# First GAT aggregation on one core: VectorE takes two of the five PSUM banks of every finished head, ScalarE the other three

## The chip, the cores and the metric

The kernel runs on one core of one Trainium2 chip. The metric is device time in microseconds (us), the median of the runs. A core has five engines with queues of their own: TensorE (PE, the matmuls; PEld is its weight load), VectorE (DVE), ScalarE (ACT), GpSimd (POOL) and SyncE (SP, which here only starts transfers). They meet through semaphores: an instruction raises a semaphore when it is done, and another engine's queue waits for a value.

## The reference, cut to what matters

A graph with 1250 nodes and 20000 edges goes through two residual blocks with a layernorm each. The first block is three graph attention layers with four heads of 192 channels, side by side, so twelve heads in all:

```python
def gat_conv(x, src, dst, W, a_src, a_dst, b):
    h = (x @ W).reshape(N, H, C)                      # N 1250, H 4, C 192
    e = leaky_relu(as_n[src] + ad_n[dst], 0.2)
    p = exp(e - segment_max(e, dst)[dst])
    s = segment_sum(p, dst)
    alpha = p / (s[dst] + 1e-16)
    out = segment_sum(alpha[:, :, None] * h[src], dst)
    return out.reshape(N, H * C) + b
xs = [relu(gat_conv(x1, src, dst, W, a_s, a_d, b)) for three sets of weights]
x = layernorm(x + relu(concat(xs) @ W_out + b_out))
```

The second block is two more attention layers. The change touches only the aggregation (the last two lines of gat_conv) of the first block.

## The kernel before

The edges are kept as a dense matrix of counts: CT holds, for ten tiles of 125 source nodes, how many edges go to each of the 1250 destinations. The sum over the edges of a head is then a product of a 1250 x 1250 matrix p with the head's rows h. The stage is the function aggregate_layer0. Its loop has ITERS = 6 iterations of two heads (hh = 0 and 1; together 384 columns, PAIR), each of 10 source tiles, so 20 steps g an iteration and 120 blocks in all.

- For a block, ScalarE makes two 125x1250 exponentials (L1081: e<-first_room,col for the first head of a pair, e<-uv,col for the second, each of which it announces by exp_ready). VectorE takes their maximum (L1119) and multiplies its cut-off value by the counts (L1124), which gives p. TensorE multiplies the ten 125x125 pieces of p with h_in (125x193: 192 channels and a column of ones, which gives the divisor s); each of the ten f32 products shows as two records in the trace, so 20 a block, and 200 a head (L1183). p has RING = 4 slots, e as well: VectorE can be up to four blocks ahead of TensorE.
- The ten destination tiles of a head gather in PSUM in p_o, two tiles to a bank, BANKS = 5 banks, over all ten blocks. The first matmul that a new head puts into a bank waits until that bank has been read out (bank_free).
- When a head is finished, VectorE works out the divisors (the helper divisors): adds 1e-16 and takes the reciprocal, for banks 0 and 1 when TensorE has finished those (banks_done), then for banks 2 to 4 when the whole head is done (L1108 and L1112, twice each). In its queue this stands behind the p of the second block of the next head (g == NT + 1, and g == 1 of the next iteration).
- ScalarE reads the ten tiles out, times their reciprocal, into res (leave_head, L1051), each two tiles raising bank_free by one. In its queue this stands behind the exponentials of the fourth block of the next head. Tiles 0 to 3 wait for the first divisors, tiles 4 to 9 for the second.
- In the first head of a pair (blocks g = 1, 3, 5) TensorE also turns the finished pair round by 10 transposes each time (turn, L1165, into p_t), and ScalarE adds the bias and applies relu behind g = 5, 7, 9 (keep, L1066); the exponentials that follow in ScalarE's queue come after it. SP stores the result (L1008). At the very end VectorE does the last third (L1144).
- The last head of the stage is an exception before the change: there ScalarE reads out only BY_ACT = 6 tiles, and VectorE the tiles 6 to 9 (L1138), with the semaphore last_left.
- VectorE also does work for a later stage in between: in 16 of the 120 blocks, every seventh (g + 20i = 4, 11, 18, ...), two reductions of 128x768 (L653, wa_by). 

The order within an engine is written out by hand; there is no planner.

Of the kernel before, what the change touches and what calls it, by code (L numbers as in the profile page):

```python
# [10 lines left out]
ALU = mybir.AluOpType  # L11
# [7 lines left out]
NT = N // T  # L19
# [9 lines left out]
H0, C0 = 4, 192  # L29
CONVS = 3  # L30
PAIR = 2 * C0
# [884 lines left out]
def aggregate_layer0(nc, core, h_rows, col_src, bias, turned_rows, w2, a2, w_out):  # L916
# [4 lines left out]
    ITERS = CONVS * H0 // 2  # L921
    STEPS = 2 * NT
    BANKS = 5
    FIRST = 2
    CW = PAIR // 128
    RING = 4
    with ExitStack() as ctx:
        sb, pb, sem = core.tools(ctx)
# [6 lines left out]
        res = sb("res", [T, NT, PAIR], F32)  # L935
        sums = sb("sums", [T, 2, NT], F32)
# [6 lines left out]
        p_o = p_all[0:T]  # L943
# [10 lines left out]
        sum_steps = sem("sum_steps")  # L954
        bank_free = sem("bank_free")
        turned = sem("turned")
        out_ready = sem("out_ready")
        stored = core.turned0_stored
        last_left = sem("last_left")
        last_out = sem("last_out")  # L960
        mask_saved = sem("mask_saved")
        ahead_in = sem("ahead_in")
        weighed = ScoreWeights(nc, sb, sem, "wa2_by", 2, D // 2, 2, K1, K1, 1)
        BY_ACT = 6

        def place(i, c):

# [68 lines left out]
        @block.scalar  # L1036
        def _(act):
            a = nc.scalar
            for c in range(CW):
                a.sem_inc(stored[c], 16)  # L1040
            a.sem_inc(bank_free, BANKS)

            def leave_head(i, hh, tiles=NT):

                act.wait_ge(turned, i * CW + CW)
                for d in range(tiles):
                    if d == 0:
                        act.wait_ge(sum_steps, (i * 2 + hh) * 4 + 2)
                    if d == 2 * FIRST:
                        act.wait_ge(sum_steps, (i * 2 + hh) * 4 + 4)  # L1050
                    last = a.activation(res[:, d, hh * C0:(hh + 1) * C0], p_o[:, d // 2, (d % 2) * 256:(d % 2) * 256 + C0],  # L1051
                                        ACT.Copy, scale=sums[:, 1, d:d + 1])
                    if d % 2:
                        last.then_inc(bank_free, 1)

            def keep(i, c):
                if i == 0 and c == 0:
                    act.wait_ge(bias_in, 16)
                    act.wait_ge(core.uv_late, all_uv)
                    act.wait_ge(core.h0_stored[0], all_h)  # L1060
                    act.wait_ge(core.h0_late, 64)
                act.wait_ge(turned, i * CW + (c + 1 + CW))

                wait_apart(act, stored[c], i * 16 + 16)
                for b, k in ((0, 4), (1, 4), (2, 2)):
                    last = a.activation(out_f[:, c, 4 * b * T:(4 * b + k) * T], place(i, c)[:, b, 0:k * T], ACT.Relu,  # L1066
                                        bias=b_col[:, bass.ds(i, 1), c])
                last.then_inc(out_ready, 1)

            def body(i, first):  # L1070
                for g in range(STEPS):
                    hh, s = divmod(g, NT)
                    if s == 0:
                        if g == 0:
                            wait_apart(act, core.first_uv_in if first else uv_in[0], 64 if first else i * 64)
                        else:
                            wait_apart(act, uv_in[1], i * 64 + 64)

                    wait_apart(act, p_ready, i * STEPS + (g + 1))
                    for kind in range(2):  # L1080
                        last = a.activation(e[:, g % RING, kind, :], uv[hh][:, kind, :], ACT.Exp,  # L1081
                                            bias=col_src[kind][:, bass.ds(i * 2 + hh, 1), s])
                    last.then_inc(exp_ready, 1)
                    if g == NT + 3:
                        leave_head(i, 0)
                    if g == 3 and not first:
                        leave_head(i - 1, 1)
                    if g in (5, 7, 9) and not first:
                        keep(i - 1, (g - 5) // 2)

            every_iteration(act, body)
            leave_head(ITERS - 1, 1, BY_ACT)
            for c in range(CW - 1):
                keep(ITERS - 1, c)

        @block.vector
        def _(dve):
            v = nc.vector
            v.sem_inc(p_ready, RING)
            v.sem_inc(exp_ready, 2 * NT)  # L1100

            def divisors(i, hh):
                for n, (b0, b1) in enumerate(((0, FIRST), (FIRST, BANKS))):
                    if n == 0:
                        dve.wait_ge(banks_done, i * 2 + hh + 1)
                    else:
                        dve.wait_ge(p_used, i * STEPS + ((hh + 1) * NT + 2 * NT))
                    v.tensor_scalar(sums[:, 0, 2 * b0:2 * b1].rearrange("p (b n) -> p b n", n=2),  # L1108
                                    p_o[:, b0:b1, :].rearrange("p b (n c) -> p b n c", n=2)[:, :, :, C0],
                                    1e-16, None, ALU.add).then_inc(sum_steps, 1)  # L1110
                    dve.wait_ge(sum_steps, (i * 2 + hh) * 4 + 2 * n + 1)
                    v.reciprocal(sums[:, 1, 2 * b0:2 * b1], sums[:, 0, 2 * b0:2 * b1]).then_inc(sum_steps, 1)  # L1112

            def body(i, first):
                for g in range(STEPS):
                    hh, s = divmod(g, NT)
                    dve.wait_ge(exp_ready, i * STEPS + (g + 1 + 2 * NT))

                    v.tensor_tensor(e[:, g % RING, 0, :], e[:, g % RING, 0, :], e[:, g % RING, 1, :], ALU.max).then_inc(more_ready, 1)  # L1119
                    dve.wait_ge(more_ready, i * STEPS + (g + 1))  # L1120

                    dve.wait_ge(p_used, i * STEPS + (g + 1 + 2 * NT - RING))

                    v.scalar_tensor_tensor(p[:, g % RING, :], e[:, g % RING, 0, :], 1.0, CT[:, s, :],  # L1124
                                           ALU.min, ALU.mult).then_inc(p_ready, 1)
                    if (i * STEPS + g) % 7 == 4 and (i * STEPS + g) // 7 < K1:
                        k = (i * STEPS + g) // 7
                        weighed.reduce(dve, k, lambda kind, j: core.wa2[:, k, kind:kind + 1])
                    if g == NT + 1:
                        divisors(i, 0)  # L1130
                    if g == 1 and not first:
                        divisors(i - 1, 1)

            every_iteration(dve, body)
            divisors(ITERS - 1, 1)
            dve.wait_ge(sum_steps, ITERS * 8)
            for d in range(BY_ACT, NT):
                last = v.tensor_scalar(res[:, d, C0:PAIR], p_o[:, d // 2, (d % 2) * 256:(d % 2) * 256 + C0], sums[:, 1, d:d + 1],  # L1138
                                       None, ALU.mult)
            last.then_inc(last_left, 1)  # L1140
            dve.wait_ge(turned, ITERS * CW + CW)
            dve.wait_ge(stored[CW - 1], ITERS * 16)
            for b, k in ((0, 4), (1, 4), (2, 2)):
                last = v.tensor_scalar(out_f[:, CW - 1, 4 * b * T:(4 * b + k) * T], p_t[:, b, 0:k * T],  # L1144
                                       b_col[:, ITERS - 1, CW - 1:CW], 0.0, ALU.add, ALU.max)
            last.then_inc(last_out, 1)

        @block.tensor
        def _(pe):
# [1 line left out]
            nc.tensor.sem_inc(turned, CW)  # L1151

            def turn(i, c):
                if i == ITERS - 1:
                    if c == 0:
                        pe.wait_ge(bank_free, i * (2 * BANKS) + 2 * BANKS + BY_ACT // 2)
                        pe.wait_ge(last_left, 1)
                    if c == 2:
                        pe.wait_ge(out_ready, i * CW + 1)
                elif c:  # L1160
                    pe.wait_ge(out_ready, i * CW + c)
                else:
                    pe.wait_ge(bank_free, i * (2 * BANKS) + 3 * BANKS)
                for d in range(NT):
                    last = nc.tensor.transpose(place(i, c)[:, d // 4, (d % 4) * T:(d % 4 + 1) * T],  # L1165
                                               res[:, d, c * 128:(c + 1) * 128], ident[0:T, 0:T])
                last.then_inc(turned, 1)

            def body(i, first):
                for g in range(STEPS):  # L1170
# [7 lines left out]
                    for d in range(NT):  # L1178
                        b, n = divmod(d, 2)
                        if s == 0 and n == 0:  # L1180

                            pe.wait_ge(bank_free, i * (2 * BANKS) + (BANKS * hh + b + 1))
                        last = nc.tensor.matmul(p_o[:, b, n * 256:n * 256 + C0 + 1], p[:, g % RING, d * T:(d + 1) * T],  # L1183
                                                h_in[hh][:, s, 0:C0 + 1], start=(s == 0 and n == 0), stop=(s == NT - 1),
                                                skip_group_check=True)
# [1620 lines left out]
```

## Time and profile before

| | before |
|---|---|
| median of 3 runs | 1889.95 us (1888.43 to 1895.02) |
| profiled execution | 1893.19 us, of which the span on the core 1891.5 us |
| PE, PEld | 1801.7 us (95%), 1742.3 us (92%) |
| VectorE | 1454.5 us (77%) |
| ScalarE | 981.8 us (52%) |
| POOL | 130.7 us (7%) |
| stage of the change | about 430 to 862 us of the span |

The profile is of one execution. An idle time is put down to what ended it. The chain of waits that ended last shows only the last 129 us of the span, which says nothing of this stage; the stage has to be read from its own stretch of the trace.

### The profile page before, as it was taken

The numbers are of one execution on the slowest core, as the hardware profiler recorded it, in microseconds if no ns is written. First come the engines' busy times: TensorE is split into PE (matmuls) and PEld (weight loads), VectorE is DVE, ScalarE is ACT, GpSimd is POOL, SyncE is SP. The second block draws the span as 40 slices with busy tenths as digits, with TensorE's granted clock in tenths as the row PEclk, the third lists the DMA queues.
The fourth block names the chain that finished last, engine by engine and source line by source line (L and its number), as shares of the span: only waits on it lengthen the run. The fifth ranks groups of instructions, "written<-read, shape, count | busy, mean of one in ns | idle before, by whom it ended". The sixth has DMA issues, their size and how long they took to land. (4 is left out here: it accounts for less than half of the span.)

```text
span 1891.5 us, 30185 instructions
## 1 busy us (share of the span) xinstructions
PE 1801.7 (95%) x11151; PEld 1742.3 (92%) x11151; DVE 1454.5 (77%) x2514; ACT 981.8 (52%) x1535; POOL 130.7 (7%) x133
## 2 busy tenths in 40 slices
PE   7999899997999999997999899989999998999898
PEld 6877699997999999996999899989999998999898
DVE  7888599998888988984645549658999995356766
ACT  5766421217898898874211232236677764232633
POOL 3110201201000000000011111100000000000000
PEclk9999899999999999998999999989999998999999
DMA  4221345454464535538654385572442408444302
GB/s 128 71 63 54 99 107 152 102 137 118 130 147 106 124 92 118 137 61 204 187 177 147 106 234 172 152 202 84 140 139 79 141 28 247 123 130 123 99 11 82
DMA packets 179272, 234.11 MB, mean 124 GB/s; under 512 B 75943, under 2 KB 151655, under 8 KB 178889
## 3 DMA queue, kind: packets, MB, share of 16 engines
q1 hardware_dynamic: 170407, 202.98, 39.6%
q0 software_dynamic: 7984, 27.24, 5.1%
q10 hardware_dynamic: 748, 2.10, 0.4%
q8 instruction: 85, 1.39, 0.3%
q14 instruction: 48, 0.39, 0.1%
HBM read 167.27 MB, written 65.00 MB: 123 GB/s over the span
## 5 line engine op out<-in xcount | busy, mean ns | idle before, releaser
L1849 PE MATMUL p_o<-p_hi,h_parts 125*128 125x416 f32 (+1 forms) x960 | 277.1, 356 | 9.4 <-DMA h_parts<-h_rows 7.8
L1183 PE MATMUL p_o<-first_room,p 125*125 125x193 f32 x1200 | 202.0, 329 | 10.4 <-DVE p L1124 7.5
L1183 PEld LDWEIGHTS p_o<-first_room,p 125*125 125x125 f32 x1200 | 197.2, 189 | 11.9 <-issue 11.4
L1183 PE MATMUL p_o<-h_in,p 125*125 125x193 f32 x1200 | 199.8, 329 | 2.1 <-ACT res L1051 2.1
L1183 PEld LDWEIGHTS p_o<-h_in,p 125*125 125x125 f32 x1200 | 197.6, 189 | 3.6 <-issue 2.4
L1849 PEld LDWEIGHTS p_o<-p_hi,h_parts 125*128 125x128 f32 x960 | 182.3, 190 | 16.1 <-DMA h_parts<-h_rows 8.3
L800 DVE CUSTOM_DVE_ANT_0 max_junk<-src_row,G 125x1250 bf16<-125x1250 f32 x120 | 184.8, 1611 | 3.7 <-ACT src_row L838 1.6
L1119 DVE TENSOR_TENSOR e<-e 125x1250 f32<-125x1250 f32 x120 | 174.3, 1452 | 17.2 <-ACT e L1081 17.1
L904 PE MATMUL p_h<-pw_hi,x1T 128*125 128x384 f32 x720 | 187.3, 341 | 0.0
L1124 DVE SCALAR_TENSOR_TENSOR p<-e,CT 125x1250 f32<-125x1250 f32 x120 | 175.3, 1461 | 4.6 <-PE p_o L1183 0.4
L1519 PE MATMUL p_h<-pw_hi,x2T 128*125 128x256 f32 (+1 forms) x960 | 175.1, 284 | 0.4 <-DVE h_out L1475 0.4
L1849 PE MATMUL p_o<-p_lo,h_parts 125*128 125x416 f32 (+1 forms) x480 | 170.4, 355 | 0.0
L1081 ACT ACTIVATE e<-first_room,col 125x1250 f32<-125x1250 f32 x120 | 151.0, 1344 | 3.9 <-DVE p L1124 2.5
L1081 ACT ACTIVATE e<-uv,col 125x1250 f32<-125x1250 f32 x120 | 149.0, 1349 | 1.2 <-DVE p L1124 1.2
L1519 PEld LDWEIGHTS p_h<-pw_hi,x2T 128*125 128x125 f32 x960 | 148.2, 187 | 0.7 <-DVE h_out L1475 0.7
L1519 PE MATMUL p_h<-pw_lo,x2T 128*125 128x256 f32 (+1 forms) x480 | 135.7, 283 | 0.0
L2120 PE MATMUL p_y<-fw_hi,f_hi 128*125 128x384 f32 x360 | 123.4, 343 | 10.4 <-DVE fw_lo L2044 10.4
L904 PEld LDWEIGHTS p_h<-pw_hi,x1T 128*125 128x125 f32 x720 | 131.6, 188 | 1.2 <-POOL pw_lo L781 1.2
L2120 PE MATMUL p_y<-fw_hi,f_lo 128*125 128x384 f32 x360 | 122.9, 341 | 0.0
L2120 PE MATMUL p_y<-fw_lo,f_hi 128*125 128x384 f32 x360 | 122.9, 341 | 0.0
L904 PE MATMUL p_h<-pw_lo,x1T 128*125 128x384 f32 x360 | 122.5, 340 | 0.0
L2401 PE MATMUL p_y<-fw_hi,f_hi 128*125 128x386 f32 x320 | 111.2, 347 | 11.1 <-DVE fw_lo L2301 5.6
(292 smaller groups left out, 3730.0 us busy)
## 6 DMA issues: line engine op xcount, KB each, us to landing
f_raw<-turned SPq DMA_DIRECT2D x40, 500.0 KB, 8.9
h_parts<-h_rows SPq DMA_DIRECT2D x40, 448.0 KB
turned<-tail_room SPq DMA_DIRECT2D x18, 625.0 KB, 6.6
G<-turned SPq DMA_DIRECT2D x20, 562.5 KB
h_rows<-tail_room SPq DMA_DIRECT2D x22, 424.4 KB
h_rows<-h_out SPq DMA_DIRECT2D x16, 560.0 KB
h_rows<-tail_room SPq DMA_DIRECT2D x14, 560.0 KB
first_room<-in_w_gat POOLq DMA_DIRECT2D x36, 192.0 KB, 2.7
```

Of the source, the lines that this page charges most:

```text
L800: v.tensor_tensor_reduce(out=junk[:, t % 2, :], in0=src_row[:, h % 2, :], in1=G[:, t, :], scale=1.0, scalar=NO_EDGE, op0=ALU.subtract, op1 ...
L904: last = nc.tensor.matmul(p_h[:, (u * NT + t) % 4, 0:width], xp[:, k, at], wp[:, u, k, :], start=(k == 0 and n == 0), stop=(k == KD - 1 an ...
L1081: last = a.activation(e[:, g % RING, kind, :], uv[hh][:, kind, :], ACT.Exp, bias=col_src[kind][:, bass.ds(i * 2 + hh, 1), s])
L1119: v.tensor_tensor(e[:, g % RING, 0, :], e[:, g % RING, 0, :], e[:, g % RING, 1, :], ALU.max).then_inc(more_ready, 1)
L1124: v.scalar_tensor_tensor(p[:, g % RING, :], e[:, g % RING, 0, :], 1.0, CT[:, s, :], ALU.min, ALU.mult).then_inc(p_ready, 1)
L1183: last = nc.tensor.matmul(p_o[:, b, n * 256:n * 256 + C0 + 1], p[:, g % RING, d * T:(d + 1) * T], h_in[hh][:, s, 0:C0 + 1], start=(s == 0 ...
L1519: last = nc.tensor.matmul(p_h[:, n % 4, 0:width], xp[:, k, at], wp[:, q % 2, k, 0:width], start=(k == 0 and j == 0), stop=(k == KD - 1 and ...
L1849: last = nc.tensor.matmul(p_o[:, bank(n, c), 0:w], h[:, s, kind, cols].bitcast(F32R), pp[:, g % RING, 0:w], start=(s == 0 and j == 0), sto ...
L2120: last = nc.tensor.matmul(p_y[:, t % 2, half, 0:CW], fp[:, n % 2, kk, :], wp[:, k, cols], start=(k == 0 and j == 0), stop=(k == KO - 1 and ...
L2401: last = nc.tensor.matmul(p_y[:, t % 2, 0:CW + 2], fp[:, m % 2, kk, :], wp[:, k, :], start=(k == 0 and j == 0), stop=(k == K1 - 1 and j == 2))
```

## The change

In every finished head, not only in the last one, ScalarE reads out the six tiles of banks 0 to 2, and VectorE the four tiles of banks 3 and 4, right behind the second reciprocal. ScalarE counts its banks in bank_free, VectorE its own in bank_left, and TensorE waits for the one or the other by the bank's number. The special case of the last head and last_left are gone.

```diff
+        ACT_BANKS, DVE_BANKS = BY_ACT // 2, BANKS - BY_ACT // 2
...
-            a.sem_inc(bank_free, BANKS)
-
-            def leave_head(i, hh, tiles=NT):
+            a.sem_inc(bank_free, ACT_BANKS)
+
+            def leave_head(i, hh):
 
                 act.wait_ge(turned, i * CW + CW)
-                for d in range(tiles):
+                for d in range(BY_ACT):
...
-            leave_head(ITERS - 1, 1, BY_ACT)
+            leave_head(ITERS - 1, 1)
...
+            v.sem_inc(bank_left, DVE_BANKS)
...
                     v.reciprocal(sums[:, 1, 2 * b0:2 * b1], sums[:, 0, 2 * b0:2 * b1]).then_inc(sum_steps, 1)
+                dve.wait_ge(turned, i * CW + CW)
+                dve.wait_ge(sum_steps, (i * 2 + hh) * 4 + 4)
+                for d in range(BY_ACT, NT):
+                    last = v.tensor_scalar(res[:, d, hh * C0:(hh + 1) * C0], p_o[:, d // 2, (d % 2) * 256:(d % 2) * 256 + C0],
+                                           sums[:, 1, d:d + 1], None, ALU.mult)
+                    if d % 2:
+                        last.then_inc(bank_left, 1)
...
             divisors(ITERS - 1, 1)
-            dve.wait_ge(sum_steps, ITERS * 8)
-            for d in range(BY_ACT, NT):
-                last = v.tensor_scalar(res[:, d, C0:PAIR], p_o[:, d // 2, (d % 2) * 256:(d % 2) * 256 + C0], sums[:, 1, d:d + 1],
-                                       None, ALU.mult)
-            last.then_inc(last_left, 1)
...
             def turn(i, c):
-                if i == ITERS - 1:
-                    if c == 0:
-                        pe.wait_ge(bank_free, i * (2 * BANKS) + 2 * BANKS + BY_ACT // 2)
-                        pe.wait_ge(last_left, 1)
-                    if c == 2:
-                        pe.wait_ge(out_ready, i * CW + 1)
-                elif c:
+                if c == 0:
+                    pe.wait_ge(bank_free, (i * 2 + 3) * ACT_BANKS)
+                    pe.wait_ge(bank_left, (i * 2 + 3) * DVE_BANKS)
+                elif i < ITERS - 1:
                     pe.wait_ge(out_ready, i * CW + c)
-                else:
-                    pe.wait_ge(bank_free, i * (2 * BANKS) + 3 * BANKS)
+                elif c == 2:
+                    pe.wait_ge(out_ready, i * CW + 1)
...
-                            pe.wait_ge(bank_free, i * (2 * BANKS) + (BANKS * hh + b + 1))
+                            if b < ACT_BANKS:
+                                pe.wait_ge(bank_free, (i * 2 + hh) * ACT_BANKS + b + 1)
+                            else:
+                                pe.wait_ge(bank_left, (i * 2 + hh) * DVE_BANKS + b - ACT_BANKS + 1)
```

## Rows read from the trace of the kernel before

**Rows 1.** The stage: span, busy PE, PEld, DVE, ACT, POOL, then clock, DMA, GB/s.
```profile
430.00:862.00 432.00, 417.83 (x2580) 414.00 (x2580) 378.56 (x357) 361.47 (x407) 16.17 (x23) 0.99 0.48 113
```

**Rows 2.** Waits in 430 to 862 us: who for whom, sum, times, longest.
```profile
DVE sums L1108 <- PE p_o L1183: 28.3, 15, 7.6
DVE e L1119 <- ACT e L1081: 17.1, 10, 5.9
PE p_o L1183 <- ACT res L1051: 5.0, 4, 2.1
PEld p_o L1183 <- ACT res L1051: 1.7, 7, 0.2
```

**Rows 3.** Timeline of PE: start, duration, count, idle before it, releaser.
```profile
472.90 34.59 PE L1183 MATMUL p_o<-h_in,p 125*125 125x193 f32 x200 [2.12 <-ACT res L1051]
...
613.38 33.04 PE L1183 MATMUL p_o<-h_in,p 125*125 125x193 f32 x200
647.39 6.77 PE L1183 MATMUL p_o<-first_room,p 125*125 125x193 f32 x40 [0.96 <-ACT res L1051]
...
753.31 33.05 PE L1183 MATMUL p_o<-h_in,p 125*125 125x193 f32 x200
786.19 6.91 PE L1183 MATMUL p_o<-first_room,p 125*125 125x193 f32 x40
```

**Rows 4.** Timeline of DVE and ACT between iterations 2 and 3.
```profile
644.66 1.46 DVE L1124 SCALAR_TENSOR_TENSOR p<-e,CT 125x1250 f32<-125x1250 f32 x1
646.04 0.16 DVE L1108 TENSOR_SCALAR sums<-p_o 125x4 f32<-125x4 f32 x1
...
646.51 3.23 ACT L1051 ACTIVATE res<-p_o,sums 125x192 f32<-125x192 f32 x10 [5.19 <-DVE sums L1112]
646.66 0.19 DVE L1112 RECIPROCAL sums<-sums 125x6 f32<-125x6 f32 x1
646.77 1.42 DVE L1119 TENSOR_TENSOR e<-e 125x1250 f32<-125x1250 f32 x1
```

**Rows 5.** Groups in 430 to 862 us: count, busy us, mean ns, idle before.
```profile
L653 DVE CUSTOM_DVE_ANT_1 wa_by_junk<-wa_by_w,wa_by_a 128x768 bf16<-128x768 f32 x32 | 29.3, 952 | 0.5 <-DMA wa_by_w<-in_w 0.5
```

**Rows 6.** Timeline of DVE between iterations 4 and 5.
```profile
784.43 0.16 DVE L1108 TENSOR_SCALAR sums<-p_o 125x4 f32<-125x4 f32 x1
```

**Rows 7.** Timeline of ACT, DVE and PEld from 600 to 615 us, iteration 2.
```profile
600.62 1.61 ACT L1066 ACTIVATE tail_room<-p_t,b_col 128x500 f32<-128x500 f32 x3 [1.10 <-PE p_t L1165]
604.70 1.46 DVE L1119 TENSOR_TENSOR e<-e 125x1250 f32<-125x1250 f32 x1 [1.78 <-ACT e L1081]
611.62 0.16 DVE L1108 TENSOR_SCALAR sums<-p_o 125x4 f32<-125x4 f32 x1 [1.09 <-PE p_o L1183]
613.89 1.42 DVE L1119 TENSOR_TENSOR e<-e 125x1250 f32<-125x1250 f32 x1
614.79 6.34 PEld L1183 LDWEIGHTS p_o<-h_in,p 125*125 125x125 f32 x39 [0.24 <-ACT res L1051]
```

**Rows 8.** Timeline of DVE between iterations 0 and 1, and at the stage's end.
```profile
505.57 0.16 DVE L1108 TENSOR_SCALAR sums<-p_o 125x4 f32<-125x4 f32 x1 [2.49 <-PE p_o L1183]
...
855.79 1.39 DVE L1138 TENSOR_SCALAR res<-p_o,sums 125x192 f32<-125x192 f32 x4
```

**Rows 9.** Timeline of PE: two other idle times of this size.
```profile
857.33 1.26 PE L1165 MATMUL p_t<-ident,res 125*128 125x125 f32 x10 [2.00 <-DVE res L1138]
...
1613.24 0.41 PE L2401 MATMUL p_y<-fw_hi,f_hi 128*125 128x386 f32 x1 [2.42 <-DVE f_lo L2296]
```

**Rows 10.** Busy time by stretch, as in rows 1, behind four idle times.
```profile
473.90:476.90 3.00, 3.00 (x11) 3.00 (x10) 2.96 (x3) 3.00 (x7) 0.00 (x0) 0.50 0.86 234
648.40:651.40 3.00, 3.00 (x21) 3.00 (x20) 2.96 (x3) 3.00 (x7) 0.00 (x0) 1.00 0.72 235
858.30:861.30 3.00, 2.26 (x21) 2.03 (x20) 0.00 (x0) 2.57 (x5) 0.00 (x0) 1.00 0.02 5
1614.24:1617.24 3.00, 3.00 (x11) 3.00 (x10) 1.02 (x3) 0.00 (x0) 0.00 (x0) 0.50 0.98 259
```

More of the change, by code:

```diff
@@ L958, in aggregate_layer0 @@
         stored = core.turned0_stored
-        last_left = sem("last_left")
+        bank_left = sem("bank_left")
         last_out = sem("last_out")
```

## The prediction

> **What bounds the kernel now.** The change touches one stage, so I read the trace by stage, and not by the whole span's shares (VectorE 77%, ScalarE 52%), which average over other stages. The busy time of the stage comes first [rows 1]: of 432 us TensorE is busy 417.8, VectorE 378.6, ScalarE 361.5. TensorE is the bound, but VectorE has only some 12% to spare, and ScalarE 16%. The sum of waits comes next [rows 2]: TensorE waits for ScalarE's read-outs (line 1051) for 5.0 us in 4 places, and its weight load for 1.7 us more in 7. That is all the change can win here, 6.7 us. VectorE waits 28.3 us for TensorE and 17.1 us for exponentials: that is the slack on which an addition to VectorE has to draw. Last the timeline [rows 3, 4, 7], for the one question that matters: when a head is done, who is late?
>
> There are two kinds of head change. Behind the first head of a pair VectorE is early: at 611.62 it has waited 1.09 us for TensorE, and TensorE goes on at 613.38 without an idle time [rows 3, 7]. Behind the second head it is late. At 646.04 it starts the divisors straight from its last p, with no wait [rows 4]; ScalarE starts at 646.51, has the second tile out at about 646.51 + 0.31 + 0.43 = 647.25 (ten tiles in 3.23 us), and TensorE starts at 647.39, having been idle 0.96 us [rows 3]. So from VectorE's divisors to TensorE's start it is 1.35 us, and that chain runs through bank 0: first divisors, tiles 0 and 1. It is seen at the ends of iterations 1, 2 and 3 (one row of the three stands). At the end of iteration 4 it is nearly level: divisors at 784.43, TensorE goes on at 786.19 with no idle row [rows 3, 6].
>
> **The change part by part.**
>
> *ScalarE's four tiles taken away* (0.31 us each, 1.3 us a head). The tiles are those of banks 3 and 4. The wait at the late change ends with tile 1, in bank 0, and the small wait of 0.24 us in the other heads [rows 7] ends with tiles 4 and 5, in bank 2: it is 0.64 us of matmuls for two banks after the head's start. Both stay with ScalarE, behind the same divisors. Banks 3 and 4 are reached by TensorE some 2 us after its start, and were free by then already: ScalarE frees a bank in 0.62 us, TensorE fills one in 33.04/50 = 0.66 us. Gain on TensorE: 0. ScalarE's later exponentials come 1.3 us earlier, but no one waits for them there: VectorE's waits for exponentials are in the first head of a pair, behind ScalarE's bias step, which itself waited 1.10 us for TensorE's transposes [rows 7]. Gain: 0.
>
> *VectorE's four tiles added* to 11 more heads (the twelfth, the last of the stage, has them already). Four take 1.39 us [rows 8]. Before, the next maximum started 0.08 us ahead of the recorded end of the second reciprocal (646.66 + 0.19 against 646.77) [rows 4]; a read-out that waits for that reciprocal can't, so I take 1.45. The bounds are 1.39, and 1.75 if in the midst of the stage they do not overlap (four of 0.41, and 0.1 for the waits), for the row is from a moment in which TensorE is still. The waits on turned and sum_steps find their values there, the first one long ago. Queued behind them on VectorE are the next block's maximum and p; TensorE has two finished blocks then (6.6 us of matmuls), VectorE needs 1.45 + 2.9 us for the next, so no block comes late. What comes late is the next divisors, when VectorE has no slack on the way to them.
>
> *First heads of a pair (five).* VectorE has 1.78 us of waiting for the exponentials of the last block but one before the divisors [rows 7], set by TensorE's transposes through the bias step, so 1.45 us are swallowed; and behind that there are another 1.09 us of waiting. Cost 0. Iteration 5 has two reductions in that head and only just fits into these two. The end of iteration 0 has 2.49 us of waiting [rows 8]: cost 0.
>
> *Second heads with two pairs of reductions on the way (iterations 1, 2, 3).* PE starts at 613.38, VectorE goes on at 613.89 and has no wait until the divisors at 646.04. Now it goes on at 615.34 and is there at 647.49; TensorE starts at 647.49 + 1.35 = 648.84 in place of 647.39. All 1.45 us come through, and the idle time grows from 0.96 to 2.41 us. Three times 1.45 = 4.35 us.
>
> *Second head with one pair (iteration 4).* A pair of reductions costs 29.3/16 = 1.8 us [rows 5]. By the same path VectorE is there 0.51 + 32.15 - 1.8 = 30.9 us after TensorE's start at 753.31, so at 784.2 (it began at 784.43), now at 785.6, and TensorE starts at 787.0 in place of 786.19. The small wait in bank 2 goes (6.91 against 6.77 us for 40 records [rows 3]). Net 0.65 us. The ends of iteration 0's first head and of the last head stay as they are.
>
> Without the clock the sum is 4.35 + 0.65 = +5.0 us (bounds 3 x 1.39 + 0.5 = 4.7 and 3 x 1.75 + 0.95 = 6.2).
>
> *The clock.* The head that starts at 472.90 behind an idle time of 2.12 us takes 34.59 us for its 200 records, against 33.04 for the same head of iteration 2 [rows 3], and the granted clock behind it is 0.50, that is 1.2 instead of 2.4 GHz; behind 0.96 us of idle it stays at 1.00 [rows 10]. So one fall costs 1.55 us. The three idle times grow to 2.41 us, from the size that left the clock alone to the size at which it fell. Of the other idle times near that, 2.42 us was followed by 0.50, and 2.00 us, in front of two short runs of transposes, by 1.00 [rows 9, 10]. Two fell of three, and the nearest in size and surroundings (dense matmuls on both sides) both fell: 0.8 for each. Three falls are likeliest: 3 x 1.55 = +4.65 us. The Trainium skill (TensorE: Matmul & The Clock Gate, section on HAM oscillation) gives as its rule that the clock is lost only behind longer idle times than any of these. The trace does not agree, at 2.12 and 2.42 us; by the page the sum would stay without this term.
>
> Together +9.65 us. The profiled execution would go from 1893.19 (span 1891.5, and 1.7 around it) to 1902.8. That execution is 3.2 us over the median, inside the runs' spread, so I put the difference on the median: 1889.95 + 9.65 = **1899.6 us**.
>
> **The rivals.**
> - *Fewer falls.* One or two of the three: +6.5 to +8.1 us, 1896.5 to 1898.1. Chance 0.27.
> - *The clock stands,* which is where the page's rule leads: VectorE's lateness is all, +5.0, 1894.95. For it speaks the 2.00 us that left the clock at 1.00. Chance 0.10.
> - *The other side: the read-out itself is what TensorE waits for.* If a head change waits for all five banks and not for bank 0, two engines at once end it sooner, and the waits on line 1051 go: up to -6.7 us, 1883.3. It decides from the point where TensorE's start follows the tenth tile. In the profile it follows the second by 0.14 us, while the tenth ends at 649.74, so this has 0.06, and most of that for a small part of the gain.
> - *VectorE's lateness is swallowed also in second heads,* through ScalarE's 1.3 us. That needs a wait of VectorE for exponentials between 613.89 and 646.04, and the trace has none; -1 to +3, about 1891. Chance 0.07.
> - *First heads become late as well,* if the read-out takes over 2 us beside TensorE's writes: 1.4 us more in four heads, and more falls: +15, 1905. Chance 0.05.
>
> **How the numbers follow.** Forecast 0.45, rivals 0.27, 0.10, 0.06, 0.07, 0.05. About 0.3% (5.7 us) is what a measurement of this kernel can tell from no change. Slower by more: 0.45 + 0.27 + 0.05, less 0.05 for one fall, which lies close to the bound: 0.72. Within: 0.25. Faster: 0.03. The range leaves out the last rival and the two with gains: from 1893.5 (no fall, less the scatter) to 1904.0 (three falls with the upper bound of the read-out, 6.2 + 4.65 = 10.9, and 3 us of scatter).
>
> **What would show it.** In the profile after: four VectorE instructions from p_o to res in each of twelve heads, at a pitch near 0.33 us; ScalarE's 72 of them; TensorE's idle time 2.4 us in three places and 0.8 us in one, at the ends of iterations 1 to 4, and none new behind first heads; granted clock 0.50 behind the three, and heads of 35 us there; VectorE's waits for TensorE and for exponentials smaller by together some 10 us. The prediction is wrong if the idle times stay at 0.96 us, if the clock stays at 1.00, or if the read-outs take over 0.5 us each.

## The result and the profile after

| | before | after |
|---|---|---|
| median of 9 runs | 1893.17 us (1888.43 to 1896.81) | 1901.23 us (1897.59 to 1905.12) |
| ratio | | 1.0046 (95% interval 1.0034 to 1.0058), that is +6.4 to +11.0 us |
| profiled execution, its span | 1893.19, 1891.5 us | 1901.74, 1900.0 us |
| VectorE, ScalarE busy | 1454.5, 981.8 us | 1469.5, 969.9 us |

The change makes the kernel slower by 8 to 9 us, 0.46%; the interval does not reach down to no change. It does what it says: VectorE has 48 read-outs in place of 4, ScalarE 72 in place of 116. The stage from its first matmul to the next stage's first grew from 432.7 to 440.2 us, +7.4 of the +8.5 us between the two spans.

The busy time of the stage's stretch in the kernel after, columns as in rows 1, and two stretches behind idle times of TensorE:

```profile
430.00:862.00 432.00, 416.83 (x2550) 413.42 (x2550) 391.66 (x396) 345.70 (x355) 16.17 (x23) 0.98 0.46 113
650.00:653.00 3.00, 3.00 (x10) 3.00 (x11) 2.96 (x5) 3.00 (x6) 0.00 (x0) 0.50 0.86 245
...
723.50:726.50 3.00, 3.00 (x21) 3.00 (x20) 2.97 (x3) 3.00 (x5) 0.00 (x0) 1.00 0.87 240
```

VectorE's busy time went up by 13.1 us in this stretch, ScalarE's down by 15.8. The two were at 378.6 and 361.5 [rows 1] and are further apart now: VectorE was the fuller one already. The timeline of TensorE in the kernel after tells the rest (start, duration, records, idle time before and its releaser):

```profile
472.37 32.91 PE L1187 MATMUL p_o<-h_in,p 125*125 125x193 f32 x200 [0.86 <-ACT res L1052]
...
576.73 8.45 PE L1187 MATMUL p_o<-first_room,p 125*125 125x193 f32 x40 [2.49 <-ACT res L1052]
...
614.37 33.05 PE L1187 MATMUL p_o<-h_in,p 125*125 125x193 f32 x200
649.90 8.34 PE L1187 MATMUL p_o<-first_room,p 125*125 125x193 f32 x40 [2.48 <-ACT res L1052]
...
722.96 6.77 PE L1187 MATMUL p_o<-first_room,p 125*125 125x193 f32 x40 [2.48 <-ACT res L1052]
...
792.69 6.77 PE L1187 MATMUL p_o<-first_room,p 125*125 125x193 f32 x40 [0.73 <-ACT res L1052]
...
864.97 2.29 PE L1166 MATMUL p_o<-ident,res 125*128 125x125 f32 x10
```

The three idle times of 0.96 us [rows 3] are now 2.48 us, and there is a fourth of 0.73 us where there was none. Behind two of the four the first 40 records take 8.4 in place of 6.77 us: the granted clock there is 0.50, that is 1.2 GHz. Behind the third of 2.48 us it stayed at 1.00.

What VectorE and ScalarE do at such a place, and at the end of the first head of the same iteration (lines 1110 and 1114 are the divisors, 1118 VectorE's read-out, 1052 ScalarE's, 1128 the next block's maximum):

```profile
605.69 1.46 DVE L1128 TENSOR_TENSOR e<-e 125x1250 f32<-125x1250 f32 x1 [1.78 <-ACT e L1082]
612.61 0.16 DVE L1110 TENSOR_SCALAR sums<-p_o 125x4 f32<-125x4 f32 x1 [1.10 <-PE p_o L1187]
```

```profile
614.77 0.19 DVE L1114 RECIPROCAL sums<-sums 125x6 f32<-125x6 f32 x1
615.00 0.73 ACT L1052 ACTIVATE res<-p_o,sums 125x192 f32<-125x192 f32 x2 [0.56 <-DVE sums L1114]
615.07 1.39 DVE L1118 TENSOR_SCALAR res<-p_o,sums 125x192 f32<-125x192 f32 x4
...
615.78 1.27 PEld L1187 LDWEIGHTS p_o<-h_in,p 125*125 125x125 f32 x8 [0.24 <-ACT res L1052]
616.38 1.45 DVE L1128 TENSOR_TENSOR e<-e 125x1250 f32<-125x1250 f32 x1
```

```profile
648.56 0.16 DVE L1110 TENSOR_SCALAR sums<-p_o 125x4 f32<-125x4 f32 x1
...
649.03 1.98 ACT L1052 ACTIVATE res<-p_o,sums 125x192 f32<-125x192 f32 x6 [5.19 <-DVE sums L1110]
...
649.31 1.46 DVE L1118 TENSOR_SCALAR res<-p_o,sums 125x192 f32<-125x192 f32 x4
649.87 3.33 PEld L1187 LDWEIGHTS p_o<-first_room,p 125*125 125x125 f32 x11 [2.75 <-issue]
```

In the first head VectorE's waits at 605.69 and 612.61 are 1.78 and 1.10 us, as before (1.78 and 1.09 [rows 7]): the addition was swallowed by then. In this head the clock had fallen, which gave VectorE time as well. Where it stood, in the first head of iteration 4, the waits for exponentials were 1.18 and 1.78 us before, and one of 1.68 us is left; from start to start of TensorE this head takes 35.95 us, before 35.96. Before, then after:

```profile
729.43 1.46 DVE L1119 TENSOR_TENSOR e<-e 125x1250 f32<-125x1250 f32 x1 [1.18 <-ACT e L1081]
...
737.03 1.46 DVE L1119 TENSOR_TENSOR e<-e 125x1250 f32<-125x1250 f32 x1 [1.78 <-ACT e L1081]
```

```profile
742.63 1.46 DVE L1128 TENSOR_TENSOR e<-e 125x1250 f32<-125x1250 f32 x1 [1.68 <-ACT e L1082]
```

Over the stretch VectorE's waits for TensorE and for exponentials shrank from 28.3 and 17.1 us [rows 2] to 22.4 and 13.9, together by 9.1. The small wait of the weight load in bank 2 is also the same 0.24 us, and it ends with ScalarE's read-out; VectorE's banks come later and nobody waits for them. In the second head VectorE goes on 2.01 us behind TensorE's start (614.37 to 616.38) and not 0.51 [rows 3, 7], has no wait on the way, and reaches the divisors 34.19 us behind it (648.56), in place of 32.66. TensorE starts 1.34 us later, at 649.90.

The working by heads, from start to start of TensorE, after against before: ends of iterations 1, 2, 3: +1.53, +1.52, +1.52; end of iteration 4: +0.90, less 0.14 for the wait in bank 2. That is +5.3 us of lateness. Falls of the clock: +1.68 and +1.58 behind two of the three places, -1.68 because the fall behind rows 3's 2.12 us did not come this time (the very first head, 35.69 in place of 34.67 us, was slower by a longer stretch at half clock, and the idle time behind it only 0.86 us), and +0.7 for the last transposes (2.29 us for ten, in place of 1.23). With -0.2 from the very first head and its wait, and +0.1 at the end of the last head, that is the +7.4.

### The profile page after: what moved, and what is told of

Its sections match the earlier page's. It is cut to its first block and busy times, and to the rows that moved or that the text cites. A ratio compares the mean times of both kernels' runs of the same rounds, so it can differ in the third digit from the quotient of the medians.

```text
span 1900.0 us, 30203 instructions
## 1 busy us (share of the span) xinstructions
PE 1804.1 (95%) x11151; PEld 1744.7 (92%) x11151; DVE 1469.5 (77%) x2558; ACT 969.9 (51%) x1491; POOL 131.0 (7%) x133
## 3 DMA queue, kind: packets, MB, share of 16 engines
q8 instruction: 85, 1.39, 0.3%
## 5 line engine op out<-in xcount | busy, mean ns | idle before, releaser
L1187 PE MATMUL p_o<-first_room,p 125*125 125x193 f32 x1200 | 206.1, 334 | 15.7 <-ACT res L1052 8.2
L1187 PEld LDWEIGHTS p_o<-first_room,p 125*125 125x125 f32 x1200 | 201.4, 192 | 17.2 <-issue 17.0
L1128 DVE TENSOR_TENSOR e<-e 125x1250 f32<-125x1250 f32 x120 | 174.5, 1455 | 14.0 <-ACT e L1082 13.9
```

## The experiments

Theory: the only cost is VectorE's lateness at the divisors, where it has no slack on its way, plus what TensorE's clock loses behind the longer idle times; relieving ScalarE is worth nothing. Rivals: TensorE waits for the read-out as a whole; or reading PSUM from two engines costs in itself; or the clock plays no part. Ratios are to the kernel before, run beside each, with their 95% intervals. A fall of the clock means that the granted clock behind an idle time of TensorE is 0.50, in place of 1.00.

**e1_relief_only.** Only the relief of ScalarE: the kernel leaves out VectorE's read-outs in eleven heads. In addition it sets their tiles to zero once at the start (not shown).

```diff
                 dve.wait_ge(sum_steps, (i * 2 + hh) * 4 + 4)
+                if (i, hh) != (ITERS - 1, 1):
+                    v.sem_inc(bank_left, DVE_BANKS)
+                    return
                 for d in range(BY_ACT, NT):
```

> The kernel after, but VectorE's four read-outs of a head are left out in the first eleven heads (tiles 6 to 9 of res stay zero there, so part of the result is missing); banks 3 and 4 are handed back right behind the second reciprocal. ScalarE keeps its six tiles, so only the relief of ScalarE is left of the change. My theory (VectorE's lateness at the divisors is the whole cost, ScalarE's relief is worth nothing): TensorE's idle time at the ends of iterations 1 to 3 is 0.96 us as before, the time is that of the kernel before within 2 us. Rival (TensorE waits for the read-out of the whole head): the idle times go below 0.3 us, the time is 3 to 7 us under the kernel before.

Measured: 0.9999 (0.9983 to 1.0016), no change within 3 us. TensorE's timeline at the end of iteration 2, with VectorE's next maximum:

```profile
645.35 1.46 DVE L1134 TENSOR_TENSOR e<-e 125x1250 f32<-125x1250 f32 x1
...
645.92 2.36 PE L1193 MATMUL p_o<-first_room,p 125*125 125x193 f32 x13 [1.22 <-ACT res L1053]
```

ScalarE has 40% less to read out, and the kernel is not faster: the relief is worth nothing, and the first rival falls. The idle time is 1.22 and not the 0.96 us that I had expected. Of these 0.26 us the waits and the raise of the semaphore that stayed make 0.21: at the end of the first head the next maximum starts 0.32 us behind the start of the second reciprocal (612.06 to 612.38), before 0.11.

**e2_extra_only.** VectorE's time alone: the kernel before, and VectorE spends 1.38 us in SBUF (not shown: the buffer extra is set to zero once at the start).

```diff
                     v.reciprocal(sums[:, 1, 2 * b0:2 * b1], sums[:, 0, 2 * b0:2 * b1]).then_inc(sum_steps, 1)
+                if (i, hh) != (ITERS - 1, 1):
+                    n = i * 2 + hh + 1
+                    dve.wait_ge(spent, n)
+                    v.tensor_tensor(extra[:, 1, :], extra[:, 0, :], extra[:, 0, :], ALU.max).then_inc(spent, 1)
```

> The kernel before, ScalarE reads out all ten tiles as there, and VectorE does one additional maximum of 1210 columns in SBUF (about 1.4 us) behind the second reciprocal of the first eleven heads, whose result nobody uses. My theory: the same as the kernel after, idle times of 2.4 us at the ends of iterations 1 to 3 and about 0.8 us at the end of iteration 4, +5.0 us and 1.55 us more for each fall of the clock, so +5 to +10 us. Rival (it is the reading of PSUM by VectorE, or two engines reading it at once, that costs): idle times 0.96 us, time of the kernel before.

Measured: 1.0047 (1.0032 to 1.0062), which is the kernel after's 1.0046, with no change to who reads PSUM.

```profile
649.97 3.23 ACT L1053 ACTIVATE res<-p_o,sums 125x192 f32<-125x192 f32 x10 [5.18 <-DVE sums L1111]
650.06 1.38 DVE L1119 TENSOR_TENSOR extra<-extra 125x1210 f32<-125x1210 f32 x1
...
650.84 3.34 PE L1190 MATMUL p_o<-first_room,p 125*125 125x193 f32 x19 [2.29 <-ACT res L1053]
```

The idle times are 2.29, 2.29, 2.28 and 0.54 us. The rival of PSUM falls: idle times of 0.96 us and the time of the kernel before were its sign, and VectorE's time costs as much when VectorE spends it away from PSUM.

**e3_one_bank and e4_three_banks.** The dose.

```diff
-        BY_ACT = 6
+        BY_ACT = 8      # e3; in e4: 4
```

> The kernel after with VectorE taking one bank (two tiles) of each head in place of two, ScalarE eight tiles. VectorE's addition is 0.33 + 0.41 + 0.06 = 0.8 us. My theory: idle times of 0.96 + 0.8 = 1.76 us at the ends of iterations 1 to 3, 0.1 us or none at the end of iteration 4, +2.4 us over the kernel before, and 1.55 for each fall of the clock; at 1.76 us I expect fewer falls than at 2.41, one or two: +2.4 to +5.5. Last head: ScalarE reads eight tiles there too, some 0.3 us later. Rival (the cost is not proportional to the tiles, but comes with the second waiting engine): +8 us as in the kernel after.

> The kernel after with VectorE taking three banks (six tiles), ScalarE four. VectorE's addition is 5 x 0.33 + 0.41 + 0.06 = 2.1 us. My theory: idle times of 0.96 + 2.1 = 3.1 us at the ends of iterations 1 to 3 and 1.4 us at the end of iteration 4, so 3 x 2.1 + 1.3 = +7.6 us over the kernel before, and with three falls of the clock +12.2 us. Rival (cost not proportional to the tiles): +8 us as in the kernel after.

Measured: one bank 1.0018 (1.0008 to 1.0029), three banks 1.0083 (1.0056 to 1.0110). TensorE behind iteration 2, first of one bank, then of three:

```profile
648.70 6.77 PE L1187 MATMUL p_o<-first_room,p 125*125 125x193 f32 x40 [1.84 <-ACT res L1052]
```

```profile
654.91 2.04 DVE L1118 TENSOR_SCALAR res<-p_o,sums 125x192 f32<-125x192 f32 x6
...
655.51 6.77 PE L1187 MATMUL p_o<-first_room,p 125*125 125x193 f32 x40 [3.05 <-ACT res L1052]
```

Idle times of 0.96, 1.84, 2.48 and 3.05 us for zero, one, two and three banks: 0.88 us for the first bank, 0.64 and 0.57 for the next two. So 0.6 us is the price of two more tiles, and some 0.25 us that of having the block of read-outs at all, as e1 shows too. With one bank the clock fell behind none of the three places (I had expected one or two falls), and +3.4 us (1.5 to 5.5) fits 3 x 0.88 and a little. With three banks +15.7 us (10.6 to 20.8) is above my 12.2, inside the interval. The stage alone grew by 15.6 us in the profile. The lateness is 8.0 of them, near my 7.6, and there were two falls in the three places and not three, 3.4 us. What I had left out is the very first head change (an idle time of 3.52 us, and a head of 35.98 in place of 34.59 us behind it, together 2.7 us) and the end of the stage (an idle time of 2.72 us before the last transposes, and those partly at half clock, together 1.5 us). The heads themselves take 33.13 in place of 33.05 us: bank 2 is VectorE's now, and TensorE's weight load waits 0.32 us for it, where it waited 0.24 us for ScalarE's read-out.

**e5_before_moved.** The kernel before, with only the reductions for the later stage in other places.

```diff
-                    if (i * STEPS + g) % 7 == 4 and (i * STEPS + g) // 7 < K1:
-                        k = (i * STEPS + g) // 7
+                    if i * STEPS + g in REDUCE_AT:
+                        k = REDUCE_AT.index(i * STEPS + g)
```
```diff
+        REDUCE_AT = (16, 24, 28, 36, 44, 48, 56, 64, 68, 76, 84, 88, 96, 104, 108, 116)
```

> The kernel before; only the places of VectorE's 16 reductions for the later stage are changed: none in the first head, two in each later first head of a pair (behind the blocks 4 and 8), one in each second head (behind block 16) in place of two in three of them. My theory (TensorE is late where VectorE reaches the divisors late, and that is where two reductions lie on its way through a head without slack): the idle times at the ends of iterations 1 to 3 fall from 0.96 to 0, that at the end of the very first head from 2.12 us to at most 0.4, so -5 us, -6.5 us with the clock's fall behind 2.12 us: 0.25 to 0.35% faster than the kernel before. Rival (the idle times belong to ScalarE's read-out, not to VectorE's place): idle times and time as before.

Measured: 0.9968 (0.9954 to 0.9981), 6 us faster than the kernel before. TensorE at the end of the very first head and of iteration 1:

```profile
469.12 33.05 PE L1184 MATMUL p_o<-h_in,p 125*125 125x193 f32 x200
...
570.97 6.90 PE L1184 MATMUL p_o<-first_room,p 125*125 125x193 f32 x40
```

No idle time is left at a head change in the whole stage. This shows the cause from the other side: the same read-outs, the same divisors, the same number of instructions, only VectorE is there in time. It is the fastest kernel of this study.

**e6_after_moved.** The same for the kernel after.

```diff
+        REDUCE_AT = (4, 13, 17, 24, 28, 44, 48, 64, 68, 84, 88, 104, 108, 112, 114, 116)
```

> The kernel after with the reductions placed so that the second heads of iterations 1 to 4 hold none (first head one, second head of iteration 0 two, five first heads two each, last head three). My theory: VectorE gains 3.6 us or 1.8 us on its way to the divisors there against 1.45 us of read-outs, so the idle times at the ends of iterations 1 to 4 are all gone, and with them the falls of the clock: 8 to 11 us under the kernel after, 1 to 4 us under the kernel before; the last head may end up to 0.8 us later. Rival (the split read-out costs in itself, in every head): it stays 3 us or more over the kernel before.

Measured: 0.9988 (0.9975 to 1.0001), 11 us under the kernel after. The idle times behind iterations 1 to 4 are gone, but not all that I expected went:

```profile
505.25 6.77 PE L1188 MATMUL p_o<-first_room,p 125*125 125x193 f32 x40 [2.30 <-ACT res L1053]
...
834.20 6.80 PE L1188 MATMUL p_o<-h_in,p 125*125 125x193 f32 x40 [0.42 <-DVE p L1134]
841.70 10.07 PE L1188 MATMUL p_o<-h_in,p 125*125 125x193 f32 x60 [0.69 <-DVE p L1134]
```

In the second head of iteration 0 the read-out (1.5) and a second pair of reductions (1.8) stood against a slack of 2.49 us [rows 8]; that slack I had read from a profile in which TensorE ran this head 1.7 us slower by the clock (34.59 against 32.91 us here), and so much less was there. In the last head, which holds three pairs of reductions, TensorE waits twice for p, 1.1 us together, where I had allowed 0.8. The result is in the range, by a sum that was off in these two places; against the kernel before it is no clear gain. That the split read-out costs 3 us or more in every placing is refuted. The 4 us between this kernel and e5's are about the size of these idle times (2.30 + 0.42 + 0.69); a better placing of the reductions was not tried.

**e7_fill, e8_after_again, e9_fill_again.** TensorE waits busily: the kernel after, with transposes of the identity in the three waits. e8 is the kernel after itself, beside e9.

```diff
                     pe.wait_ge(p_ready, i * STEPS + (g + 1 + RING))
+                    if g == 0 and i in (2, 3, 4):
+                        pe.wait_ge(out_ready, (i - 1) * CW)
+                        for n in range(FILL):       # 18
+                            nc.tensor.transpose(p_t[0:T, 0, 0:T], ident[0:T, 0:T], ident[0:T, 0:T])
```

> The kernel after; at the ends of iterations 1 to 3 TensorE does 18 transposes of the identity (about 1.9 us) into a free bank of p_t in front of its wait, so it waits busily; nothing of the computation is changed. My theory (part of the cost is the fall of TensorE's clock behind 2.4 us of idle time): the new head starts at the same moment as in the kernel after, the granted clock stays at 1.00 there, each of the three heads takes its 6.77 us for the first 40 records and not 8.4, and the time is 1.55 us less for each fall avoided: 3 to 5 us under the kernel after, +4 to +5 over the kernel before. Rival (the clock plays no part): time of the kernel after.

> The kernel after once more, on the same chip and in the same rounds as the next two, so that they can be compared with it. VectorE's lateness (idle times of 2.48, 2.48, 2.48 and 0.73 us, +5.3 us) is the same in every run; the falls of the clock are not. So far the clock fell behind five of nine idle times of 2.1 to 2.5 us in this stage. My theory: +5.3 and 1.7 to 3 us for the falls, ratio 1.0035 to 1.0050.

> The same kernel as e7_fill (18 transposes of the identity in the three waits of TensorE), now beside the kernel after. Theory: the new heads start as late as in the kernel after, the clock stays at 1.00 behind them, 1.7 to 5 us under the kernel after. Rival (the clock is worth nothing in the sum of many runs): within 1 us of the kernel after.

Measured: filled 1.0020 (1.0009 to 1.0031) and again 1.0016 (1.0003 to 1.0030); the kernel after beside the second 1.0050 (1.0035 to 1.0065). TensorE in e7, end of iteration 2:

```profile
644.85 2.12 PE L1183 MATMUL p_t<-ident 125*125 125x125 f32 x18
647.40 6.80 PE L1192 MATMUL p_o<-first_room,p 125*125 125x193 f32 x40 [0.43 <-ACT res L1053]
```

From the second head's start (611.97) it is 35.43 us to 647.40, in the kernel after 35.53: the head starts only 0.1 us earlier than there. But its first 40 records take 6.80 and not 8.4 us, in all six filled places. So VectorE's lateness is all but untouched, and a part of the cost is gone: 4.9 and 6.4 us by the ratios, 5.3 and 3.9 by the medians (of the two pairs only the second ran side by side). That the clock plays no part is refuted: the intervals of e8 and e9 do not overlap. The size is less sure. In the profiles of the kernel after (twice) the clock fell behind 3 of 6 idle times of 2.48 to 2.49 us, which is 1.5 x 1.65 = 2.5 us a run; the gain by the ratios is larger, with an interval of 3 to 4 us to either side.

**e10_before_fill.** The same trick for the one fall in the kernel before.

```diff
+                    if first and g == NT:
+                        for n in range(FILL):       # 16
+                            nc.tensor.transpose(p_t[0:T, 0, 0:T], ident[0:T, 0:T], ident[0:T, 0:T])
```

> The kernel before with 16 transposes of the identity in TensorE's wait behind the very first head, where it is idle for 2.12 us. VectorE's place is unchanged, so the second head starts as late as before. Theory: only the fall of the clock behind that wait goes, which comes in some runs: -0.5 to -1.7 us, hardly more than can be measured; in the profile the second head takes 33.0 us and not 34.6. Rival (the busy wait itself delays the head): the second head starts later than 1.35 us behind VectorE's divisors.

Measured: 0.9996 (0.9986 to 1.0007), no difference that the time can tell, as expected. In the profile:

```profile
470.74 1.91 PE L1181 MATMUL p_t<-ident 125*125 125x125 f32 x16
473.68 32.94 PE L1187 MATMUL p_o<-h_in,p 125*125 125x193 f32 x200 [1.03 <-ACT res L1052]
```

The head takes 32.94 in place of 34.59 us [rows 3], the idle time before it being 1.03 and not 2.12 us. The wait itself was longer in this run (2.94 us in all), so that the two together say nothing on the total. It was VectorE that was later: it starts the divisors at 472.43, 0.9 us later than in the kernel before. TensorE follows 1.25 us behind, before 1.34 us, so the busy wait itself does not delay the head.

## Why the prediction was right, and where it was off

- *Direction and size.* 1899.6 us was forecast, 1901.2 measured, in the range of 1893.5 to 1904.0. The difference was forecast as +9.65 us and is +8.1 by the medians, +8.7 by the ratio. That the absolute number fits is in part luck: the median of before is 3.2 us higher over nine runs than over the three that I had, and that made up for a difference forecast 1.0 to 1.6 us too large.
- *ScalarE's relief: 0.* Right (e1), and for the reason given: both waits of TensorE end in banks 0 and 2, which ScalarE keeps. One figure on the way was wrong: two banks of matmuls are 2 x 0.66 = 1.3 us, not 0.64, which fits bank 2 better still (the weight load waits until 614.79, 1.41 us behind the head's start at 613.38 [rows 3, 7]).
- *VectorE's addition: 1.45 us.* Measured 1.50: the next maximum starts at 616.38, 1.61 us behind the second reciprocal's start at 614.77, before 0.11 (613.78 to 613.89). The four take the 1.39 us of rows 8 also beside a busy TensorE and ScalarE. The Trainium skill (VectorE: DVE Perf Modes, the section on the TRN2 errata) gives VectorE 120 cycles and one for each element to read from PSUM to SBUF, at 0.96 GHz. For 192 elements that is an estimate of 0.325 us. The trace agrees: one read-out takes 0.41 us and four take 1.39, so they follow each other at (1.39 - 0.41)/3 = 0.327 us.
- *First heads: 0.* Right. The wait that swallows most of the addition is an earlier one than I had named: in iteration 4 the 1.18 us are gone, and of the 1.78 us only 0.1.
- *Second heads: 3 x 1.45 + 0.65 = 5.0 us.* Measured 3 x 1.52 + 0.76 = 5.3. Right, place by place; e2 and e5 show the cause from both sides.
- *The clock: three falls of 1.55 us.* The price was right (1.68 and 1.58 us), the chance was not. I took 0.8 for each from two falls in three idle times near that size [rows 9, 10]. Over all profiles of this study idle times of 2.1 to 2.5 us ahead of a head (0.50 behind them or not) come twelve times: six falls (2.12, 2.29, 2.48, 2.49, 2.49, 2.50) and six without (2.28, 2.29, 2.30, 2.48, 2.49, 2.49). The same kernel at the same place, the end of iteration 2, had both, at 2.48 and 2.49 us. So the term is about 2.5 us (half of three, at 1.65) and not 4.65, and the likeliest case should have been one or two falls (+6.7 to +8.3). It was mis-sized by about 2 us.
- *The rule that would leave the clock alone.* The Trainium skill (TensorE: Matmul & The Clock Gate, section on HAM oscillation) would leave the clock alone behind idle times of this length. The traces do not agree with it at 2.12 to 2.50 us, and they do not support that the length alone decides: 3.05 us left it alone once (e4_three_banks), 2.12 us did not.
- *The rivals of a faster kernel and of a swallowed lateness.* Refuted by e1 and by the idle times.

## What to carry to other kernels

In this kernel the work that moved from one engine to another was paid where the receiving engine had least slack on its way to the next thing that the bound engine waits for, not by its share of busy time: seven of eleven additions of 1.4 us cost nothing, three cost all of it, one a half. Before work is split, look at the wait that is really last: it was the first bank's, and the change took over the last two. And where an engine is late now and then, look first for other work in its queue that can go to a place with slack: moving the reductions without changing any was worth 0.3%, while the three splits of the read-out with the reductions left in place (e3, the kernel after, e4) cost 0.2 to 0.8%.

## What the runs showed that I had not expected

- Behind idle times of 2.1 to 2.5 us the clock fell six times of twelve, and at the same place of the same kernel it did both. Behind six idle times of 0.96 us and four of 1.80 to 1.84 us in this stage it did not fall. The falls are not spread evenly over the places, though: of all idle times over 2 us ahead of a head (2.12 to 3.52 us), the clock fell behind all four at the end of the very first head and all four at the end of iteration 1, but behind two of eight at the ends of iterations 2 and 3, and not behind the one at the end of iteration 0 (e6). What decides it stays open. Two microseconds of useless transposes in the wait kept the clock up each time (seven of seven), three of these at the two places where it had always fallen.
- Two waits and a semaphore raise behind the reciprocal cost VectorE 0.21 us a time (e1): the next maximum starts 0.13 us behind the recorded end of the reciprocal, where it started 0.08 us ahead of it. In e2, where the wait is for a value that came long before, the next instruction still starts 0.11 us behind the reciprocal's start (649.95 to 650.06). So it is likely the wait for VectorE's own last result that costs, or the raise; the two were not tried apart.
- The idle time behind the very first head of the stage was between nothing and 3.5 us over these profiles, 2.12 in the kernel before. TensorE's first head takes from 34.4 to 35.9 us by when the clock comes back. A part of the scatter of several us between runs of the same kernel may come from such places; that was not tested.
